# A recurrence's first 32 tokens are normalised ahead of its step 0, the other columns and the skip products behind its steps

## The reference, cut to what matters

```python
def _L0_conv_ref(x, A, Bm, Cm, D, W_in, b_in, W_out, b_out, gamma, beta):
    residual = x
    h = x.transpose(0, 2, 3, 1).reshape(Bsz, Hh * Ww, C)
    mu = jnp.mean(h, axis=-1, keepdims=True)
    var = jnp.mean((h - mu) ** 2, axis=-1, keepdims=True)
    hn = (h - mu) * jax.lax.rsqrt(var + LN_EPS) * gamma + beta
    z = jnp.einsum('blc,ec->ble', hn, W_in) + b_in
    u = jnp.einsum('ble,se->bls', z, Bm)
    def step(state, u_t):
        state = jnp.tanh(state @ A.T + u_t)
        return (state, state)
    ...
    y = jnp.einsum('bls,es->ble', states, Cm) + z * D
    out = jnp.einsum('ble,ce->blc', y, W_out) + b_out
    return out + residual
```

## Time and profile before

| | |
|---|---|
| median of 3 runs | 690.57 us (690.24 to 690.89) |
| span of the profiled execution | 685.1 us |
| TensorE busy | 482.2 us (70%) |
| VectorE busy | 303.6 us (44%) |
| ScalarE busy | 321.7 us (47%) |
| mean granted TensorE clock | 0.754 |

### The profile page before, as it was taken

How to read it: one execution, slowest core, us unless ns; L and a number is a source line. 1 busy time by engine, 2 the same in 40 slices (tenths; PEclk the granted TensorE clock), 3 DMA queues, 4 the chain that set the end, 5 groups by cost and what they waited for, 6 DMA issues and landing times.

```text
span 685.1 us, 10767 instructions
## 1 busy us (share of the span) xinstructions
PE 482.2 (70%) x3952; PEld 269.5 (39%) x3953; DVE 303.6 (44%) x727; ACT 321.7 (47%) x1089; POOL 6.1 (1%) x9
## 2 busy tenths in 40 slices
PE   4653655556897689999856666666667799989733
PEld 2221222223663466766623333333332454455311
DVE  1184000005883678888833000000007887478543
ACT  3332333333573767777732333333347555655521
POOL 0000000000000000000000000000003000000000
PEclk9555555556899899999985555555559999999987
DMA  5000000000000000000000000000003110000000
GB/s 195 0 2 1 0 1 1 0 1 0 1 1 1 0 2 1 1 1 1 2 0 1 0 1 0 1 1 0 1 0 84 40 40 3 1 2 3 1 9 32
DMA packets 8381, 7.45 MB, mean 11 GB/s; under 512 B 3202, under 2 KB 8066, under 8 KB 8196
## 3 DMA queue, kind: packets, MB, share of 16 engines
q1 hardware_dynamic: 8324, 6.70, 3.3%
HBM read 4.99 MB, written 0.52 MB: 8 GB/s over the span
## 4 chain that ended last, share of the span: by engine, by line
PE 57%; DVE 16%; ACT 16%; issue 7%; DMA 1%; DVEq 1%; SPq 1%; ACTq 0%
PE ps L325 16%; ACT arena L343 11%; PE ps L303 4%; PE ps L308 3%; PE ps L652 2%; PE ps L859 2%; PE ps L822 2%; PE ps L639 2%; PE ps L635 2%; PE ps L838 2%; PE ps L666 2%; DVE arena L1384 2%; DVE arena L1393 2%; PE ps L265 2%; PE ps L826 2%
## 5 line engine op out<-in xcount | busy, mean ns | idle before, releaser
L325 PE MATMUL ps<-arena,wsb 16*16 16x16 f32 (+1 forms) x1024 | 131.3, 206 | 116.6 <-ACT arena L343 111.1
L343 ACT ACTIVATE arena<-ps 16x16 f32<-16x16 f32 (+1 forms) x512 | 96.0, 188 | 190.4 <-PE ps L325 190.4
L325 PEld LDWEIGHTS ps<-arena,wsb 16*16 16x16 f32 (+1 forms) x1024 | 76.4, 118 | 200.0 <-ACT arena L343 186.5
L349 DVE TENSOR_TENSOR X<-X,ps 128x128 f32<-128x128 f32 x16 | 4.6, 287 | 199.1 <-PE ps L308 199.1
L1081 ACT ACTIVATE arena<-ps,arena 128x128 f32<-128x128 f32 (+1 forms) x128 | 52.4, 418 | 31.0 <-DVE arena L1385 30.9
L1189 ACT ACTIVATE arena<-ps 128x512 f32<-128x512 f32 x72 | 40.8, 595 | 26.8 <-PE ps L826 24.3
L1533 DVE TENSOR_TENSOR arena<-arena,ps 128x512 f32<-128x512 f32 x64 | 42.0, 682 | 17.3 <-ACT arena L1189 13.5
L1384 DVE TENSOR_REDUCE arena<-ps 128x2 f32<-128x512 f32 (+1 forms) x48 | 33.0, 688 | 18.4 <-PE ps L635 11.0
L652 PE MATMUL ps<-wsb,arena 128*128 128x128 f32 x192 | 30.4, 281 | 12.1 <-DVE arena L1393 12.1
L639 PE MATMUL ps<-arena 128*128 128x256 f32 x128 | 36.1, 406 | 0.0
L1393 DVE TENSOR_TENSOR arena<-arena 128x512 f32<-128x512 f32 x48 | 33.2, 691 | 1.7
(11 more groups left out here) (276 smaller groups left out, 750.2 us busy)
## 6 DMA issues: line engine op xcount, KB each, us to landing
wsb<-weights SPq DMA_DIRECT2D x1, 2060.5 KB, 9.8
arena<-w SPq DMA_DIRECT2D x20, 64.0 KB
arena<-xn SPq DMA_DIRECT2D x9, 128.0 KB, 2.5
wsb<-weights SPq DMA_DIRECT2D x1, 549.5 KB, 4.3
X<-x SPq DMA_DIRECT2D x1, 512.0 KB, 3.4
out<-arena SPq DMA_DIRECT2D x2, 256.0 KB, 2.3
arena<-w_biases SPq DMA_DIRECT2D x20, 17.0 KB
csb<-consts SPq DMA_DIRECT2D x1, 128.0 KB, 9.6
```

Of the source, the lines that this page charges most:

```text
L325: nc.tensor.matmul(step_columns(k, rows, r), w_state, states[0:rows, :, :, t].rearrange("p g j -> p (g j)"), start=False, stop=True, skip_ ...
L343: nc.scalar.activation(states[0:rows, :, :, t + 1].rearrange("p g j -> p (g j)"), step_columns(t // STEP_BANK, rows, t % STEP_BANK), func) ...
```

## The change

X is cut into 8 chunks of 32 tokens (128 columns each). Ahead of step 0 only chunk 0 is normalised, on ScalarE as before. For chunks 1 to 7, TensorE issues the mean and variance products behind steps of the recurrence, in two halves of 64 columns (`chunk_products`); VectorE takes 1/sqrt(variance) by a bit trick and three Newton rounds. The skip products become 32 products of one group of images and one chunk (`skip_product`), each behind the step after that group's `bank_out`, and waiting until that is written; they share the chunk's bank. The bias `u_b`, a column of 16 values in SBUF, goes into each of the 256 tanhs as their bias operand, where 0.0 stood as a constant of the instruction, and `bias_bank` is gone. The fills move to steps 20, 23, 26 and 29, in both recurrences; each `bank_out` now raises its semaphore. The mask program stands behind the seven chunks on VectorE, and all adds to X behind the mask program. The diff, cut to its core:

```diff
+FILLS, OUTS, SKIPS = (20, 23, 26, 29), (4, 7, 10, 13), (5, 8, 11, 14)
+CENTRED = ((0, 1), (14, 15), (27, 28), (41, 44), (56, 57), (70, 73), (85, 86))
+VARIED = ((5, 6), (18, 19), (32, 33), (47, 48), (60, 62), (76, 79), (89, 91))
...
-            if g == G - 1:
-                mm.then_inc(s["bank out"], 1)
+            mm.then_inc(s["bank out"], 1)
+
+        def skip_product(pe, m, g):
+            group = slice(C * g, C * (g + 1))
+            bank, c0 = (m, P) if m < BANKS - 1 else (m - 1, 2 * P)
+            pe.wait_ge(s["bank out"], G * bank + g + 1)
+            nc.tensor.matmul(ps[group, bank, c0:c0 + P], g2[group, group], xnj[group, :, STEP_BANK * m:STEP_BANK * (m + 1)],
+                             start=True, stop=True).then_inc(s["L0 skip"], 1)
...
+        def chunk_products(pe, t):
+            for m in range(1, BANKS):
+                for i in range(2):
+                    js, cols = slice(2 * i, 2 * i + 2), slice(i * P // 2, (i + 1) * P // 2)
+                    if t == CENTRED[m - 1][i]:
+                        if i == 0 and m > 2:
+                            pe.wait_ge(s["L0 chunk saved"], 2 * (m - 2))
+                        nc.tensor.matmul(ps[:, 4 + m % 2, cols], W("centre"), chunk(X[:], m)[:, js, :], start=True, stop=True)\
+                            .then_inc(s["L0 chunk products"], 1)
+                    if t == VARIED[m - 1][i]:
+                        if i == 0:
+                            pe.wait_ge(s["L0 chunk saved"], 2 * m - 1)
+                        nc.tensor.matmul(ps[:, 6 + m % 2, cols], W("block"), chunk(sq[:], m)[:, js, :], start=True, stop=True)\
+                            .then_inc(s["L0 chunk products"], 1)
...
-                if r == 0 and n == 0:
-                    pe.wait_ge(s["bank biased"], k + 1)
-                if r == 0 and n == 1:
+                if r == 0:
                     pe.wait_ge(s["bank filled"], fills(n, k, G))
...
-            norm_tensor(pe, 0)
...
+            pe.wait_ge(s["normalised"], 2)
             for g in range(G):
-                bank_fill(pe, 0, 0, g, NS, u_w[:])
-
-            for h in range(2):
-                nc.tensor.matmul(ps[:, 6 + h, :], g2[:], halves(xn)[h], start=True, stop=True).then_inc(s["L0 skip"], 1)
+                mm = nc.tensor.matmul(ps[0:NS, 0, g * P:(g + 1) * P], u_w[:, C * g:C * g + NS], chunk(xn[:], 0),
+                                      start=(g == 0), stop=True, skip_group_check=True)
+            mm.then_inc(s["bank filled"], G)
...
-            recur_scalar(act, 0, NS, ACT.Tanh)
+            recur_scalar(act, 0, NS, ACT.Tanh, bias=u_b[0:NS])
...
+            variance, root, step, centred = (xc[:, i * P:(i + 1) * P] for i in range(4))
+            for m in range(1, BANKS):
+
+                dve.wait_ge(s["L0 chunk products"], 4 * m - 2)
+                if m > 1:
+                    dve.wait_ge(s["L0 chunk saved"], 2 * (m - 1))
+                link(nc.vector.tensor_copy(centred, ps[:, 4 + m % 2, 0:P]))
+                centred_j = centred.rearrange("p (j t) -> p j t", j=J)
+                nc.vector.scalar_tensor_tensor(chunk(sq[:], m), centred_j, 1.0 / C, centred_j, ALU.mult, ALU.mult)\
+                    .then_inc(s["L0 chunk saved"], 1)
+                dve.wait_ge(s["L0 chunk products"], 4 * m)
+                link(nc.vector.tensor_scalar(variance, ps[:, 6 + m % 2, 0:P], EPS, None, ALU.add))
+                link(nc.vector.tensor_scalar(root.bitcast(I32), variance.bitcast(I32), 1, None, ALU.logical_shift_right))
+                link(nc.vector.tensor_scalar(root.bitcast(I32), root.bitcast(I32), -1.0, float(0x5f3759df), ALU.mult, ALU.add))
+                for _ in range(3):
+                    link(nc.vector.tensor_tensor(step, root, root, ALU.mult))
+                    link(nc.vector.scalar_tensor_tensor(step, step, -0.5, variance, ALU.mult, ALU.mult))
+                    link(nc.vector.scalar_tensor_tensor(root, step, 1.5, root, ALU.add, ALU.mult))
+                nc.vector.tensor_tensor(chunk(xn[:], m), root.rearrange("p (j t) -> p j t", j=J), centred_j, ALU.mult)\
+                    .then_inc(s["L0 chunk saved"], 1)
```

More of the change, by code:

```diff
@@ L326, in recur_tensor @@
                                  start=False, stop=True, skip_group_check=True).then_inc(s["pre-state"], 1)
[L327 to L333, removed]
+                if n == 0 and k == 1 and r == OUTS[0]:
+                    pe.wait_ge(s["L0 weights"], 2)
+                if k > 0 and r in OUTS:
+                    bank_out(k - 1, OUTS.index(r), rows, w_out)
+                if n == 0 and k > 0 and r in SKIPS:
+                    skip_product(pe, k - 1, SKIPS.index(r))
+                if n == 0 and k == BANKS - 1 and r in FILLS:
+                    skip_product(pe, k, FILLS.index(r))
+                if n == 0:
+                    chunk_products(pe, t)
+                if k < BANKS - 1 and r in FILLS:
+                    if n == 0 and r == FILLS[0]:
+                        pe.wait_ge(s["L0 chunk saved"], 2 * (k + 1 if k < 3 else min(k + 3, BANKS - 1)))
+                    if n == 1 and STEP_BANK * (k + 1) == P and r == FILLS[0]:
                         pe.wait_ge(s["F input"], 2)
-                    bank_fill(pe, n, k + 1, (r - 17) // 3, rows, w_in)
+                    bank_fill(pe, n, k + 1, FILLS.index(r), rows, w_in)
             pe.wait_ge(s["state"], (n + 1) * T)
@@ L338, in recur_tensor, with recur_scalar @@
                 bank_out(BANKS - 1, g, rows, w_out)
-        def recur_scalar(act, n, rows, func):
+        def recur_scalar(act, n, rows, func, bias=0.0):
             for t in range(T):
@@ L343, in recur_scalar @@
                 nc.scalar.activation(states[0:rows, :, :, t + 1].rearrange("p g j -> p (g j)"),
-                                     step_columns(t // STEP_BANK, rows, t % STEP_BANK), func).then_inc(s["state"], 1)
+                                     step_columns(t // STEP_BANK, rows, t % STEP_BANK), func, bias=bias).then_inc(s["state"], 1)
         def add_bank_out(dve, n, k):
-            dve.wait_ge(s["bank out"], BANKS * n + k + 1)
+            dve.wait_ge(s["bank out"], G * (BANKS * n + k + 1))
             cols = Xj[:, :, STEP_BANK * k:STEP_BANK * (k + 1)]
@@ L1255, in _ @@
[L1255 to L1268, removed]
@@ L1269, in _ @@
-            dve.wait_ge(s["L0 skip added"], 2)
-            bias_bank(1)
+            dve.wait_ge(s["L0 folds"], 3)
+            nc.vector.tensor_copy(u_b[:], ps[:, 3, P:P + 1]).then_inc(s["L0 weights"], 1)
+            dve.wait_ge(s["1/sigma"], 2)
+            nc.vector.tensor_tensor(chunk(xn[:], 0), chunk(sq[:], 0), ps[:, 7, 0:P].rearrange("p (j t) -> p j t", j=J), ALU.mult)\
+                .then_inc(s["normalised"], 2)
+            dve.wait_ge(s["L0 folds"], 4)
+            nc.vector.tensor_tensor(g1[:], W("block"), ps[:, 2, 0:P], ALU.mult)
@@ L1286, in _ @@
             link(nc.vector.tensor_copy(acting[:], following.rearrange("p n o w -> p (n o w)")))
[L1287 to L1291, removed]
+            for m in range(BANKS):
+                dve.wait_ge(s["L0 skip"], G * (m + 1 if m < BANKS - 2 else BANKS))
+                if m < BANKS - 1:
+                    link(add_bank_out(dve, 0, m))
+                bank, c0 = (m, P) if m < BANKS - 1 else (m - 1, 2 * P)
+                nc.vector.scalar_tensor_tensor(chunk(X[:], m), ps[:, bank, c0:c0 + P].rearrange("p (j t) -> p j t", j=J), o_b[:],
+                                               chunk(X[:], m), ALU.add, ALU.add).then_inc(s["L0 chunk saved"], 1)
+            dve.wait_ge(s["L0 chunk saved"], 2 * (BANKS - 1) + BANKS)
             link(add_bank_out(dve, 0, BANKS - 1))
```

43 lines of the change are left out of this document (28 added, 15 removed).

## The result

The changed kernel takes 704.71 us (703.81 to 705.4, 4 runs), the one before 690.4 us in the same comparison (689.9 to 690.89, 4 runs). The ratio is 1.019, 95% interval [1.014, 1.023]: 14.3 us slower. The forecast was slower, at 698.5 us in a range of 695.0 to 703.0, so the direction held and the size did not.

A forecast was written before the change was run, and what follows sets the result against it. No engine was full; the bound was the recurrence's chain of TensorE product and ScalarE tanh, 0.507 us a step. Terms -10.8 - 5.2 + 23.6 + 0.3 = +7.9 us took 690.6 to 698.5 us, range 695.0 to 703.0.

The forecast's parts named there:

- The time before step 0: Folds, centring and fills ahead of the first recurrence: step 0 at 11.3 instead of 22.05 us, -10.8 us.
- The stall at step 64: First recurrence: the 5.75 us interval, waiting for bank 2's bias behind the mask program, goes with bias_bank, -5.2 us.
- The tanh's bias operand: ScalarE in the first recurrence: an SBUF bias adds 0.092 us to each of 256 steps, +23.6 us.
- The 28 chunk products: TensorE behind recurrence steps: array free 0.61 us after the step began, 0.01 us each, +0.3 us, upper bound 5.0.
- The skip products: 28 products one step behind bank_out: done inside the 0.599 us step, cost 0, at worst 1.4 us.
- VectorE's chain: From variance to xn, 4.1 us; chunk to chunk 5.6 us within at least 10 steps: cost 0, at worst 1.0.
- The sum: Whole kernel: -10.8 - 5.2 + 23.6 + 0.3 = +7.9 us, giving 698.5 us.
- Everything waits its turn: Rival: chunk products cost 5.0, skips 1.4, VectorE 0.5 us; 6.6 more than forecast, 705.1 us; chance 0.09.
- The clock did not rise: Rival on TensorE in the recurrence: clock rises to 2.4 GHz, 688 us in all steps, 696.5 in 50; chance 0.06.

The follow-up runs named there:

- e6: The kernel before, with only VectorE's mask program moved behind the biases of all banks and the adds to X up to bank 5; 688.87 us, ratio 0.994.
- e1: The changed kernel with the tanh's bias a constant 0.0 again and the input bias left out of the recurrence; 687.61 us, ratio 0.997.
- e2: The kernel before, with only the first recurrence's tanh taking its bias from a column of zeros in SBUF; 711.76 us, ratio 1.031.
- e10: The changed kernel with a second column operand, a scale of ones from SBUF, in each tanh of the first recurrence; 725.5 us, ratio 1.048.
- e3: The changed kernel with chunk products cut by image group into 56 of 32x32 weights, each reading its group's 32 rows; 697.84 us, ratio 1.011.
- e4: The changed kernel with chunk products cut into 56 of 32-wide weights, each reading all 128 rows; 707.4 us, ratio 1.026.
- e8: The changed kernel with u_b as a row of the state weights and chunk products cut into 56 of 32x32 weights; 679.15 us, ratio 0.980.
- e9: As e8, but each skip product two steps behind the bank_out it waits for, not one; 675.37 us, ratio 0.979.
- e7: The changed kernel with u_b as a 32nd row of the state weights against a row of ones in the states; 687.31 us, ratio 0.994.

## Why the prediction was right and wrong

- **The time before step 0** was forecast at -10.8, within -10.3 to -11.6. It measured -10.2, just outside: the folds ended 0.3 us later, and the fills took 1.89 us for eight passes and 0.06 until step 0 instead of 1.7.
- **The stall at step 64**, -5.2: right; no interval at a bank change is above 0.68, and e6 shows it alone.
- **The tanh's bias operand**, +23.6: right in size and in place. e1, e2 and e10 show it from three sides. This term decided the sign of the forecast.
- **The 28 chunk products**, +0.3 with an upper bound of 5.0: this is the step that failed. I had the passes right (0.227, and 0.107 for the columns), but let the product start 0.05 us after the step. It starts 0.16 after, and the next step follows 0.62 after that start instead of 0.56: 0.78 us against steps of 0.60, 28 x 0.18 = 5.0 us. The row on which I leaned priced a pass, not the hand-over from a step and back to one. e3 and e4 show that the late start and the wait belong to products that reach over all 128 rows, not to those that merely share rows with the step.
- **The skip products**, 0: right at steps of 0.60. What I wrote for steps of 0.507, that only the group that shares the step's rows pays 0.16, was half right: that one pays 0.17, but the other three pay 0.12 each. e8's chunk products on the same tiles pay nothing at these steps. e9 ties the price to standing one step behind `bank_out`.
- **VectorE's chain**, 0: right, and its 4.1 us too.
- **The sum**: -10.2 - 5.2 + 23.5 + 5.0 and 0.3 of small things are the 13.4 us of the trace, 5.5 more than forecast, 4.7 of them from the chunk products. The medians differ by 0.9 us more, the two traced spans by 3.5 more. Those 3.5 lie behind the first recurrence; but from the last tanh to the end the thirteen traces take 527.7 to 538.2 us with nearly the same work, so no run tells them from scatter.

The range left the chunk products' upper bound out, since I gave it to a rival of chance 0.09 and let the range end halfway. Price and doubt were both in one hand-over that no row showed, and there the upper bound should have weighed more. That this bound met the 5.0 us measured is in part luck: it was made of a start 0.23 us after the step and two passes of 0.273, and the trace has 0.16 and 0.62. So is the nearness of the rival *Everything waits its turn* (705.1): of its three prices only that of the chunk products was paid. The clock did not rise in the recurrence, as the section on the hardware shows. (Where that rival reads slices 2 to 9 before as 50 to 60% busy, slice 4, with the stall in it, has only a 3.)

## What to carry to other kernels

In a chain of short steps, look first at what each step's instruction gains or loses, an operand included: 0.092 us here, times 256, outweighed everything the change had won, and one more row in the matrix product that stands there anyway did the same addition for nothing (e7). Of the products hidden behind such a step, those of 32x32 weights were free, on the step's own rows too, but for the skips at steps of 0.507 us, as long as they stood only one step behind the product that they waited for; those that reached over all 128 rows never were. Four small products cost nothing where two large ones, for the same work, cost 0.18 us each. What a longer step hides comes back when the step gets shorter, as the skips did.

## What the runs showed of the hardware

The granted clock that the profile prints can be wrong until its first record. In the changed kernel the windows over the first and the second recurrence read (length, busy time of each engine, granted clock):

```profile
60.00:168.00 108.00, 69.04 (x502) 30.36 (x502) 31.87 (x149) 49.49 (x178) 0.00 (x0) 1.00 0.00 1
377.00:520.00 143.00, 87.30 (x623) 46.50 (x622) 6.82 (x16) 47.66 (x254) 0.00 (x0) 0.50 0.00 1
```

1.00 in the first, 0.50 in the second; yet the step's passes last 0.23 us as in the earlier trace rows, where 0.50 stood, and the fills' eight passes took 1.89 us, 0.21 to 0.24 for 128 columns, which is the rate of the earlier trace rows. The second passes of the fills and skip products between the steps begin 0.17 to 0.21 us after the first ones, up to the last bank; in the first fill before, at 17.41 us under a recorded 1.00, it was 0.11. So the array ran at 1.2 GHz in this recurrence too; the first record of the clock in this trace stands at 181.9 us, and up to there the row says 1.00. The same holds of the first 13 us before: there the centring's passes of 512 columns took 0.86 us under a 9. So mean clocks of 0.754 and 0.865 for the two kernels say nothing of their speed, and durations of known passes do.

The kernel before has a scatter of its own at its start, most of it from the clock. In the trace shown, the four fills took 1.71 us and the skip products 3.07. In e2, whose start is the same work, the fills took 2.56 and the skip products 3.78, and the first tanh came at 24.82 us instead of 22.32. The windows of the trace before, and then of e2:

```profile
13.10:19.70 6.60, 3.84 (x14) 1.15 (x13) 1.92 (x3) 4.36 (x6) 0.00 (x0) 1.00 0.00 0
...
18.00:24.50 6.50, 5.98 (x12) 1.67 (x12) 1.69 (x3) 0.77 (x1) 0.00 (x0) 0.50 0.00 0
```

Before, the full clock is recorded from 13.0 to 19.8 us, so over the fills, which begin at 17.41. In e2 it is recorded from 14.5 to 17.9, and the fills begin at 18.34. The passes of 512 columns follow the record: 0.86 us apart ahead of it, 0.43 to 0.48 in it, 0.86 behind it, in both. TensorE was busy with the centring when the clock rose. Ahead of the fills it stood idle for 2.6 us in both; in e2 the clock fell in that gap, in the trace before only in the skip products. Of the 2.5 us, 0.3 come from a later landing of the weights and the rest from these passes. So the -10.2 us is the difference of two traces and would have been -12.7 against e2's. The changed kernel has no products of 512 columns there, and its step 0 lay at 11.8 and 11.9 us in two runs.
